# Four-block network on one core: GpSimd rounds the third and fourth input groups of the MLP to FP4 in place of VectorE

## The chip, the cores and the metric

The kernel runs on one core of a Trainium2 chip, as one launch. A core has TensorE (matmuls and transposes, results in PSUM), VectorE, ScalarE and GpSimd (elementwise work), and SyncE, which here issues the DMAs. Each engine runs its own queue of instructions in order and waits on semaphores for the others. The metric is the device time of one execution in microseconds.

## The reference

The input `x` (32 sequences of 64 tokens, width 128) passes four residual blocks: cross attention with rotary positions, a routed FFN (2 of 8 experts), cross attention by autocorrelation, and last the MLP that the change touches. Before each stands a layer norm, and each block's result is scaled by the tanh of a gate. The MLP quantises its inputs and weights to FP4 in blocks of 16 values, and multiplies:

```python
def fp4_quant_dequant(x):
    xb = x.reshape(shape[:-1] + (shape[-1] // BLOCK, BLOCK))
    scale = jnp.max(jnp.abs(xb), axis=-1, keepdims=True) / 6.0
    scale = jnp.maximum(scale, jnp.float32(1e-12))
    xn = xb / scale
    idx = jnp.searchsorted(_MID, jnp.abs(xn))
    q = _GRID[idx] * jnp.sign(xn) * scale
    return q.reshape(shape)
def fp4_linear(x, w):
    return jnp.einsum('bsk,nk->bsn', fp4_quant_dequant(x), fp4_quant_dequant(w))
...
gate = fp4_linear(x, w_gate)          # 128 -> 352
y = fp4_linear(x, w_up)
h = jax.nn.silu(gate) * y
return fp4_linear(h, w_down)          # 352 -> 128
```

## The kernel before

All work is scheduled by hand: every engine has one written-out order of steps, and semaphores tie the orders together. The 2048 tokens are 16 tiles of 128 tokens. In the MLP the inputs are quantised in four **groups** of four tiles (512 columns of a 128-partition buffer; the code counts them from 0, so the third and the fourth are groups 2 and 3), and the rest goes in eight **pairs** of two tiles (704 columns of h), counted from 0. The last two pairs are finished as four halves.

*A group's quantisation.* `x_scale` on VectorE takes the blocks' largest magnitudes (L285), their reciprocals (L286), and shrinks the values (L290, 128x512) so that the FP4 steps become steps of a float's own rounding. ScalarE takes magnitudes (`x_magnitude`, L734). `x_round` on VectorE rounds with two instructions of the same helper, `fp4_off` (L298): max(magnitude, 1.5) minus value, and max(magnitude, 1.5) minus that. GpSimd then scales back: `fp4_scale` (L294, 32 numbers) and `fp4_unscale` (L305, 128x512) in `x_unscale`. TensorE transposes the group (`turn_x`, L1601), ScalarE copies the transposes out of PSUM.

*A pair.* TensorE makes the gate product and the up product (`gate`, `up`, both on L1607), ScalarE the SiLU (L721). VectorE multiplies the two (L1090, from PSUM), takes the blocks' maxima (L1095), their reciprocals (L1101) and shrinks h (L290, 128x704). ScalarE takes magnitudes (L728), VectorE rounds with two instructions (L298, 128x704), one step later. GpSimd unscales (L294, L305, 128x704), TensorE transposes h (L1633) and makes the down product onto the residual (L1639, L1644), ScalarE copies the result out, and SyncE stores it.

VectorE's order in the MLP is: groups 0 and 1, then `pair_step(q)` for each pair q. A step q holds the product and the shrink of pair q and the roundings of pair q - 1. Between the maxima and the reciprocals of a step stand the odd jobs: `x_round(2)` in step 1, `x_scale(3)` in step 2, `x_round(3)` in step 3; `x_scale(2)` ends step 0. GpSimd's order is a loop over q from 1: in rounds 1 and 3 the unscale of group 2 or 3, then the scale of pair q - 1, then the unscale of pair q - 1, which waits for VectorE's roundings in step q. TensorE's order is `up(q+1)`, then turn and down product of pair q - 2, then `gate(q+2)`, and in rounds 1 and 3 the transposes of group 2 or 3.

Of the kernel before, what the change touches and what calls it, by code (L numbers as in the profile page):

```python
# [15 lines left out]
ALU = mybir.AluOpType  # L16
# [89 lines left out]
def build(nc, a):  # L106
    with ExitStack() as ctx:
# [21 lines left out]
        def carve(start, *shape):  # L129
            return shaped(region[:, start:start + int(np.prod(shape))], shape)  # L130
# [61 lines left out]
        qv, qm, qd, xqT = ([carve(k + 512 * i, 4 * D) for i in range(2)] for k in range(14336, 18432, 1024))  # L192
# [33 lines left out]
        x2_tr x2_done xn_c xn_c_late xn_c_dve xf_done xf_used q_done pp_done hs_done hs_read hs_turned cf_ready corr_done corr_read  # L226
        dve_c lead_ready lead_exp lags_ready lags_turned gt_ready g_done of_done
        y1_done y1_ready o_done x3_read x3_done
        floors_set hsc_ready xsc_ready rolled_made codes_set xn_d xn_d_dve xv_done xm_done xd_done xq_done xqt_done xqt_used gate_done gu_done sg_done hh_done hv_done hm_done hd_done hq_done hq_last ht_done ht_used dn_done x4_done out_done dve_d""".split()
        m = {n: ctx.enter_context(nc.semaphore(n)) for n in names}  # L230
        x_sem = [m["ld_x0"], m["ld_x1"]]
        w_sem = [m[f"w{i}"] for i in range(6)]
# [44 lines left out]
        def blocks(z):  # L277
            return z.rearrange("p (n k) -> p n k", k=BLK)

        def spread(z, nblk):  # L280
            return z.unsqueeze(2).broadcast_to([P, nblk, BLK])
# [6 lines left out]
        def fp4_shrunk(eng, out, src, inv):  # L288

            return eng.scalar_tensor_tensor(out, src, 6.0 / FINE * (1.0 - 2.0 ** -24), inv, ALU.mult, ALU.mult)  # L290

        def fp4_scale(eng, amax, sc):

            return eng.tensor_scalar(sc, amax, FINE / 6.0, None, ALU.mult)  # L294

        def fp4_off(eng, out, mag, z):

            return eng.scalar_tensor_tensor(out, mag, 1.5, z, ALU.max, ALU.subtract)  # L298

        def fp4_round(eng, st, v, mag, diff):  # L300
            st.step(fp4_off(eng, diff, mag, v))
            return fp4_off(eng, diff, mag, diff)

        def fp4_unscale(eng, diff, sc, nblk, out):
            return eng.tensor_tensor(blocks(out), blocks(diff), spread(sc, nblk), ALU.mult)  # L305
# [47 lines left out]
        def _(pool):  # L353
# [119 lines left out]
            def x_unscale(g):  # L473
                pool.wait_ge(m["xv_done"], g + 1)
                fp4_scale(pool, xmx[g % 2], xsc[g % 2]).then_inc(m["xsc_ready"], 1)
                pool.wait_ge(m["xd_done"], g + 1)
                pool.wait_ge(m["xsc_ready"], g + 1)
                fp4_unscale(pool, qd[g % 2], xsc[g % 2], 4 * D // BLK, qv[g % 2]).then_inc(m["xq_done"], 1)
# [10 lines left out]
            def h_scale(q):  # L489

                pool.wait_ge(m["hv_done"], q + 1)
                if q >= 3:
                    pool.wait_ge(m["hq_done"], q - 2)
                fp4_scale(pool, hmx[q % 3], hsc[q % 3]).then_inc(m["hsc_ready"], 1)

            for q in range(1, WHOLE + 1):
                u = (q - 1) % 2
                if q in (1, 3):
                    x_unscale((q + 3) // 2)
                h_scale(q - 1)  # L500
                pool.wait_ge(m["hd_done"], q)
                pool.wait_ge(m["hsc_ready"], q)
                if q >= 3:
                    pool.wait_ge(m["ht_done"], q - 2)
                fp4_unscale(pool, hd[u], hsc[(q - 1) % 3], 2 * NH, hq[u].rearrange("p a n -> p (a n)")).then_inc(m["hq_done"], 1)
# [289 lines left out]
        def _(dve):  # L795
# [267 lines left out]
            def x_scale(g):  # L1063

                u = g % 2
                dve.wait_ge(m["xn_d"], 4 * g + (2 if g else 4))
                if g == 1:
                    dve.wait_ge(m["xn_d_dve"], 2)
                if g >= 2:
                    dve.wait_ge(m["xqt_done"], g - 1)  # L1070
                    dve.wait_ge(m["xsc_ready"], g - 1)
                else:
                    dve.wait_ge(m["floors_set"], 3)
                nblk = 4 * D // BLK
                src = xb[:, nblk * g:nblk * (g + 1), :]
                fp4_inverse(dve, dd, src, xmx[u], xin[u])
                fp4_shrunk(dve, blocks(qv[u]), src[:, :, 0:BLK], spread(xin[u], nblk)).then_inc(m["xv_done"], 1)

            def x_round(g):
                dve.wait_ge(m["xm_done"], g + 1)  # L1080
                fp4_round(dve, dd, qv[g % 2], qm[g % 2], qd[g % 2]).then_inc(m["xd_done"], 1)

            def pair_step(q):

                u, w, n3 = q % 2, (q - 1) % 2, q % 3
                if q < PAIRS:
                    dve.wait_ge(m["sg_done"], q + 1)
                    dve.wait_ge(m["gu_done"], q + 1)
                    rows = "p a (n k) -> p a n k"
                    dve.tensor_tensor(hh[u].rearrange("p (a n) k -> p a n k", a=2), sg[u].rearrange(rows, k=BLK),  # L1090
                                      ps[:, 3:5, 0:MLP].rearrange(rows, k=BLK), ALU.mult).then_inc(m["hh_done"], 1)
                    if q >= 3:
                        dve.wait_ge(m["hq_done"], q - 2)
                    dve.wait_ge(m["hh_done"], q + 1)
                    k = dd.mark(dve.tensor_reduce(hmx[n3], hb[u], AX, ALU.max, apply_absolute_value=True))  # L1095
                    if q in (1, 3):
                        x_round((q + 3) // 2)
                    if q == 2:
                        x_scale(3)
                    dd.after(k)  # L1100
                    dd.step(dve.reciprocal(hin[n3], hmx[n3]))  # L1101
                    fp4_shrunk(dve, hh[u], hh[u], spread(hin[n3], 2 * NH)).then_inc(m["hv_done"], 1)
                    if q == 0:
                        x_scale(2)
                if 1 <= q <= WHOLE:
                    dve.wait_ge(m["hm_done"], q)
                    if q >= 3:
                        dve.wait_ge(m["hq_done"], q - 2)
                    dd.step(fp4_off(dve, blocks(hd[w]), blocks(hm[w]), hh[w]))
                    fp4_off(dve, hd[w], hm[w], hd[w]).then_inc(m["hd_done"], 1)  # L1110
# [23 lines left out]
            for q in range(PAIRS):  # L1134
                pair_step(q)
# [673 lines left out]
```

## Time and profile before

| what | value |
|---|---|
| median of 3 timed runs | 273.46 us (272.43, 273.46, 278.04) |
| the profiled execution, whole | 271.89 us |
| its span, first to last instruction | 270.1 us |
| TensorE matmul busy | 249.0 us, 92% |
| VectorE busy | 190.2 us, 70%, 494 instructions |
| ScalarE busy | 164.3 us, 61% |
| GpSimd busy | 125.0 us, 46%, 200 instructions |
| TensorE's granted clock, mean | 0.994 |

The shares are means over the four blocks, which have different bounds; the MLP is the last stage, from about 205 us on. Times in the rows below count from the start of the span. PE is TensorE, PEld its weight loads, DVE is VectorE, ACT is ScalarE, POOL is GpSimd. In a timeline, several instructions of one line are merged into one row with their count behind "x".

### The profile page before, as it was taken

To read this page: it belongs to the slowest core of one execution; us is meant where nothing else is said; L and a number is where in the kernel's file an instruction comes from. 1 tells how busy PE (TensorE), PEld (TensorE's weight loads), DVE (VectorE), ACT (ScalarE), POOL (GpSimd) and SP (SyncE) were. 2 spreads that over 40 slices of the span, in tenths; PEclk is the share of its full clock that TensorE was granted. 3 is DMA by queue.
4 is the path that set the end of the run, shared out by engine and by line. 5 is a ranking of instruction groups with operands and counts; after the bars stand their busy time and mean duration, and the time that the engine had idled before them with its cause. 6 is when DMAs were issued, how large, how long until landed. Compare 5 with 4: busy or idle time off the path is not lost.

```text
span 270.1 us, 6349 instructions
## 1 busy us (share of the span) xinstructions
PE 249.0 (92%) x2204; PEld 197.5 (73%) x2204; DVE 190.2 (70%) x494; ACT 164.3 (61%) x382; POOL 125.0 (46%) x200
## 2 busy tenths in 40 slices
PE   8999999999798989999999999979999864999886
PEld 6656477777576868999999999765699532667675
DVE  4899588888999764352222222796686999999993
ACT  2369996666478656686566667474448683353543
POOL 4475579999601403219992220267004534252220
PEclk9999999999999999999999999999999999899999
DMA  6999100000000118876777772000000000000111
GB/s 192 380 344 410 40 4 2 2 4 0 2 2 4 31 56 340 362 290 285 290 301 287 291 296 81 0 4 0 4 0 2 1 0 0 0 21 23 39 40 40
DMA packets 12384, 30.19 MB, mean 112 GB/s; under 512 B 1088, under 2 KB 5440, under 8 KB 12224
## 3 DMA queue, kind: packets, MB, share of 16 engines
q1 hardware_dynamic: 12352, 29.78, 29.2%
q8 instruction: 18, 0.29, 0.5%
q14 instruction: 14, 0.11, 0.1%
HBM read 9.78 MB, written 1.05 MB: 40 GB/s over the span
## 4 chain that ended last, share of the span: by engine, by line
PE 58%; DVE 23%; issue 7%; ACT 5%; DMA 2%; SPq 1%; POOL 1%; DVEq 0%; ACTq 0%
PE ps L1420 12%; PE ps L1409 11%; DVE s_region L298 5%; PE ps L1252 5%; PE ps L1226 5%; PE ps L1239 4%; PE ps L1159 3%; DVE s_region L1090 3%; PE ps L1150 3%; DVE s_small L1095 2%; PE ps L1151 2%; PE ps L1262 2%; DVE s_region L290 2%; PE ps L1470 1%; DMA s_ctxT<-ctxT 1%
## 5 line engine op out<-in xcount | busy, mean ns | idle before, releaser
L635 ACT ACTIVATE s_region<-ps,s_region 128x128 f32<-128x128 f32 x144 | 41.0, 369 | 21.8 <-PE ps L1409 21.7
L965 DVE SCALAR_TENSOR_TENSOR s_ctxT<-ps,s_region,s_ctxT 128x64 f32 x72 | 18.1, 282 | 43.9 <-PE ps L1420 43.9
L1409 PE MATMUL ps<-s_region 128*128 128x128 f32 x288 | 38.2, 276 | 0.2 <-DMA s_region<-s_wall 0.2
L1420 PE MATMUL ps<-s_region 128*128 128x128 f32 x288 | 37.9, 275 | 0.0
L1409 PEld LDWEIGHTS ps<-s_region 128*128 128x128 f32 x288 | 35.0, 192 | 0.7 <-DMA s_region<-s_wall 0.3
L1420 PEld LDWEIGHTS ps<-s_region 128*128 128x128 f32 x288 | 35.0, 192 | 0.2 <-issue 0.2
L430 POOL COPY s_region<-s_xt 128x64 f32 x72 | 14.8, 236 | 31.0 <-PE ps L1409 23.3
L1607 PE MATMUL ps<-s_region 128*128 128x352 f32 x64 | 22.4, 491 | 6.2 <-DVE s_region L1090 3.9
L575 ACT COPY s_region<-ps 128x512 f32<-128x512 f32 x32 | 17.2, 592 | 15.1 <-PE ps L1239 15.1
L305 POOL TENSOR_TENSOR s_region<-s_region,s_small 128x704 f32<-128x704 f32 (+2 forms) x11 | 14.6, 1331 | 23.7 <-DVE s_region L298 23.5
L1252 PEld LDWEIGHTS ps<-s_region 128*64 128x64 f32 x512 | 16.3, 138 | 12.5 <-ACT s_region L575 10.7
L834 DVE TENSOR_REDUCE s_small<-ps 128x16 f32<-128x1024 f32 x16 | 19.6, 1225 | 8.0 <-PE ps L1226 7.9
L374 POOL TENSOR_SCALAR s_region<-s_region 128x512 f32<-128x512 f32 x16 | 24.7, 1569 | 0.1
L271 POOL TENSOR_SCALAR s_small<-s_small 128x4 f32<-128x4 f32 (+3 forms) x14 | 3.2, 231 | 44.4 <-DVE s_small L248 44.4
L1607 PEld LDWEIGHTS ps<-s_region 128*128 128x128 f32 x64 | 11.8, 198 | 13.2 <-DVE s_region L1090 5.4
L298 DVE SCALAR_TENSOR_TENSOR s_region<-s_region 128x704 f32<-128x704 f32 (+2 forms) x28 | 20.4, 728 | 0.7 <-ACT s_region L734 0.2
L842 DVE TENSOR_TENSOR s_region<-ps,s_small 128x1024 f32<-128x1024 f32 x16 | 19.5, 1216 | 0.1
L1252 PE MATMUL ps<-s_region 128*64 128x18 f32 x512 | 17.8, 212 | 1.2 <-DVE s_x L857 0.9
L1226 PE MATMUL ps<-s_region 64*64 64x512 f32 x128 | 17.4, 614 | 1.1 <-POOL s_region L374 1.1
L570 ACT ACTIVATE s_region<-s_region 128x1024 f32<-128x1024 f32 x16 | 17.0, 1063 | 0.7 <-DVE s_region L842 0.7
L1239 PE MATMUL ps<-s_par,s_region 128*128 128x128 f32 x128 | 16.7, 273 | 0.0
L273 POOL TENSOR_TENSOR s_small<-s_small,s_par 128x4 f32<-128x4 f32 (+3 forms) x14 | 16.3, 1163 | 0.0
(237 smaller groups left out, 523.3 us busy)
## 6 DMA issues: line engine op xcount, KB each, us to landing
s_region<-s_wall SPq DMA_DIRECT2D x36, 514.0 KB, 3.0
s_wall<-wall SPq DMA_DIRECT2D x8, 514.0 KB, 9.4
s_par<-par SPq DMA_DIRECT2D x1, 1280.0 KB, 10.4
s_x<-x SPq DMA_DIRECT2D x2, 512.0 KB, 6.7
out<-s_x SPq DMA_DIRECT2D x6, 128.0 KB, 1.9
s_region<-ffn SPq DMA_DIRECT2D x1, 560.0 KB, 3.6
s_ctxT<-ctxT SPq DMA_DIRECT2D x2, 256.0 KB, 4.1
s_ctxT<-ctxT SPq DMA_DIRECT2D x1, 512.0 KB, 6.6
```

The lines of the kernel that those rows point to most:

```text
L298: return eng.scalar_tensor_tensor(out, mag, 1.5, z, ALU.max, ALU.subtract)
L374: pool.tensor_scalar(kbd[g % 2][:, j, :], cols, hmask[:, j:j + 1], None, ALU.mult).then_inc(m["kbd_done"], 1)
L635: ins = act.activation(hg[j % 3][:, c, :], ps[:, j % 3, RPT * S * c:RPT * S * (c + 1)], ACT.Gelu, bias=wbuf[j % 6][:, FF + FC * D + c:FF + ...
L834: dve.tensor_reduce(mx[t % 2], scores(t % 2), AX, ALU.max).then_inc(m["mx_done"], 1)
L842: dve.tensor_tensor(ssub[t % 2], scores(t % 2), mx[t % 2].unsqueeze(2).broadcast_to([P, H, S]), ALU.subtract).then_inc(m["s_sub"], 1)
L965: dve.scalar_tensor_tensor(row, ps[:, 4 + j % 2, S * k:S * k + S], w, row, ALU.mult, ALU.add).then_inc(m["acc_done"], 1)
L1226: ins = mm(ps[S * row:S * row + S, 2 * (t % 2) + half, :], qT[rows, 2 * t + row, :], kbd[g % 2][rows, :, k:k + S], start=True, stop=True)
L1239: ins = tr(ps[:, 4 + half, P * k:P * k + P], pr[t % 2][:, c:c + P], ident)
L1252: ins = mm(ps[S * row:S * row + S, 6 + t % 2, n * c:n * c + n], pT[t % 2][:, c, S * row:S * row + S], vbd[:, 2 * t + row, c, :], start=Tru ...
L1409: ins = mm(ps[:, j % 3, RPT * S * c:RPT * S * (c + 1)], w[:, P * c:P * c + P], xg[j % 4], start=True, stop=True)
L1420: ins = mm(ps[:, 4 + j % 2, 0:RPT * S], w[:, FF + D * c:FF + D * c + D], hg[j % 3][:, c, :], start=(c == 0), stop=(c == FC - 1))
L1607: ins = mm(ps[:, 1 + 2 * n + t, 0:MLP], xqT[(q // 2) % 2][:, lo:lo + P], wguT[:, MT * P * n:MT * P * n + MLP], start=True, stop=True)
```

## The change

The two calls of `x_round` that stand inside VectorE's `pair_step` go. GpSimd gets a new function, `x_round_late`, called in rounds 1 and 3 of its loop directly before `x_unscale` of the same group. [...] Groups 0 and 1 stay on VectorE.

```diff
+            def x_round_late(g):
+
+                u, done = g % 2, 2 * (g - 2)
+                pool.wait_ge(m["xm_done"], g + 1)
+                pool.tensor_scalar(qm[u], qm[u], 1.5, None, ALU.max).then_inc(m["xr_done"], 1)
+                pool.wait_ge(m["xr_done"], done + 1)
+                pool.tensor_tensor(qd[u], qm[u], qv[u], ALU.subtract).then_inc(m["xr_done"], 1)
+                pool.wait_ge(m["xr_done"], done + 2)
+                pool.tensor_tensor(qd[u], qm[u], qd[u], ALU.subtract).then_inc(m["xd_done"], 1)
+
             for q in range(1, WHOLE + 1):
                 u = (q - 1) % 2
                 if q in (1, 3):
+                    x_round_late((q + 3) // 2)
                     x_unscale((q + 3) // 2)
                 h_scale(q - 1)
...
                     k = dd.mark(dve.tensor_reduce(hmx[n3], hb[u], AX, ALU.max, apply_absolute_value=True))
-                    if q in (1, 3):
-                        x_round((q + 3) // 2)
                     if q == 2:
                         x_scale(3)
                     dd.after(k)
```

## Rows read from the trace of the kernel before

**Rows 1.** Busy us by engine in one stretch of the MLP; then PEclk, DMA.

```profile
235.00:240.00 5.00, 4.55 (x26) 3.29 (x25) 4.83 (x7) 2.15 (x4) 3.25 (x4) 1.00 0.09 28
```

**Rows 2.** Chain of waits that ended last, from 215 us: start, us, what.

```profile
236.43 0.61 DVE s_region L298
...
237.06 0.69 DVE s_region L298
...
238.16 1.40 issue
...
265.74 0.55 PE ps L1655 x3
```

**Rows 3.** Timeline of VectorE, 221 to 257 us: start, us, line, operation.

```profile
223.05 1.41 DVE L298 SCALAR_TENSOR_TENSOR s_region<-s_region 128x512 f32<-128x512 f32 x2
224.37 0.42 DVE L1101 RECIPROCAL s_small<-s_small 128x44 f32<-128x44 f32 x1
224.83 1.52 DVE L290 SCALAR_TENSOR_TENSOR s_region<-s_region,s_small 128x704 f32<-128x704 f32 x1
226.27 1.83 DVE L298 SCALAR_TENSOR_TENSOR s_region<-s_region 128x704 f32<-128x704 f32 x2
228.01 0.88 DVE L1090 TENSOR_TENSOR s_region<-s_region,ps 128x704 f32<-128x704 f32 x1
...
230.91 0.69 DVE L290 SCALAR_TENSOR_TENSOR s_region<-s_region,s_small 128x512 f32<-128x512 f32 x1
...
234.51 0.88 DVE L1090 TENSOR_TENSOR s_region<-s_region,ps 128x704 f32<-128x704 f32 x1
...
241.31 0.88 DVE L1090 TENSOR_TENSOR s_region<-s_region,ps 128x704 f32<-128x704 f32 x1
...
243.72 0.89 DVE L290 SCALAR_TENSOR_TENSOR s_region<-s_region,s_small 128x704 f32<-128x704 f32 x1
...
246.26 0.88 DVE L1090 TENSOR_TENSOR s_region<-s_region,ps 128x704 f32<-128x704 f32 x1
...
256.17 0.88 DVE L1090 TENSOR_TENSOR s_region<-s_region,ps 128x704 f32<-128x704 f32 x1
```

**Rows 4.** Timeline of GpSimd, 221 to 257 us; in brackets idle time before.

```profile
224.54 1.06 POOL L305 TENSOR_TENSOR s_region<-s_region,s_small 128x512 f32<-128x512 f32 x1 [2.78 <-DVE s_region L298]
225.68 0.85 POOL L294 TENSOR_SCALAR s_small<-s_small 128x44 f32<-128x44 f32 x1
228.18 1.38 POOL L305 TENSOR_TENSOR s_region<-s_region,s_small 128x704 f32<-128x704 f32 x1 [1.65 <-DVE s_region L298]
229.65 0.32 POOL L294 TENSOR_SCALAR s_small<-s_small 128x44 f32<-128x44 f32 x1
```

**Rows 5.** Two lines early in the kernel (L820, L382): ns min/median/max, first and last start.

```profile
L820 DVE TENSOR_SCALAR s_region<-s_region x4: 477/480/1493, 16.7 to 17.9; 128x512 f32<-128x512 f32 x4
...
L382 POOL TENSOR_TENSOR s_region<-s_region x6: 1268/1276/1498, 9.3 to 26.4; 128x512 f32<-128x512 f32 x6
```

**Rows 6.** GpSimd's instructions by line and shape: count, busy us, mean ns.

```profile
L374 POOL TENSOR_SCALAR s_region<-s_region 128x512 f32<-128x512 f32 x16 | 24.7, 1569 | 0.1
...
L400 POOL TENSOR_TENSOR s_region<-s_region 128x512 f32<-128x512 f32 x2 | 2.6, 1280 | 0.2
```

**Rows 7.** Timeline of ScalarE, 221 to 257 us: the two groups' magnitudes.

```profile
221.40 0.63 ACT L734 ACTIVATE s_region<-s_region 128x512 f32<-128x512 f32 x1
...
233.86 0.62 ACT L734 ACTIVATE s_region<-s_region 128x512 f32<-128x512 f32 x1
```

**Rows 8.** Timeline of TensorE, 221 to 257 us: transposes, and products of pairs.

```profile
225.65 0.66 PE L1601 MATMUL ps<-s_par,s_region 128*128 128x128 f32 x4 [0.80 <-POOL s_region L305]
228.95 2.71 PE L1607 MATMUL ps<-s_region 128*128 128x352 f32 x4 [2.64 <-DVE s_region L1090]
...
252.20 2.53 PE L1607 MATMUL ps<-s_region 128*128 128x352 f32 x8
```

**Rows 9.** Busy us by engine from 228 to 232 us, columns as above.

```profile
228.00:232.00 4.00, 3.05 (x8) 1.95 (x9) 3.86 (x8) 0.28 (x1) 1.71 (x2) 0.57 0.00 0
```

More of the change, by code:

```diff
@@ L228, in build @@
         y1_done y1_ready o_done x3_read x3_done
-        floors_set hsc_ready xsc_ready rolled_made codes_set xn_d xn_d_dve xv_done xm_done xd_done xq_done xqt_done xqt_used gate_done gu_done sg_done hh_done hv_done hm_done hd_done hq_done hq_last ht_done ht_used dn_done x4_done out_done dve_d""".split()
+        floors_set hsc_ready xsc_ready rolled_made codes_set xn_d xn_d_dve xv_done xm_done xd_done xr_done xq_done xqt_done xqt_used gate_done gu_done sg_done hh_done hv_done hm_done hd_done hq_done hq_last ht_done ht_used dn_done x4_done out_done dve_d""".split()
         m = {n: ctx.enter_context(nc.semaphore(n)) for n in names}
```

## The prediction

> **What bounds the kernel now.** I read three views in this order. First the busy time by stretch: in the MLP VectorE works 4.83 of every 5.00 us while GpSimd works 3.25 [rows 1]. Second the chain of waits over the last stage: up to 265.74 us each step on it is VectorE's (or its issue), the two roundings that the change moves stand there with 0.61 and 0.69 us, and only at 265.74 does TensorE follow [rows 2]. Third the timelines of VectorE and GpSimd against each other [rows 3, 4]. The reader is to see the distance from one SwiGLU product (L1090) to the next. A plain step, 241.31 to 246.26, takes 4.95. The step with the fourth group's rounding, 234.51 to 241.31, takes 6.80. The excess of 1.85 has two parts. One is the rounding itself. The other is a stall: the shrink on L290, 0.89 alone (243.72), takes 1.52 at 224.83 because GpSimd's unscale of the inputs runs until 225.60; the chain shows the same stall again as 1.40 of "issue" at 238.16 [rows 2, 3, 4]. So the stall is 0.63 and the rounding, net of what it covered, 1.85 - 0.63 = 1.22.
>
> VectorE is the bound, so 1.22 twice, 2.4 us, looks free to take. With the stall twice it is 3.7 us. Even this upper end is 1.4% of the time, under the 2% that a measurement of this kernel can tell from no change (the three times shown lie 272.43 to 278.04).
>
> **What is removed.** Two scalar_tensor_tensor of 128x512 in each of two steps: 1.41 us for a pair [rows 3], 1.22 net as above. VectorE also no longer waits for the magnitudes of these groups.
>
> **What is added.** On GpSimd, three instructions for each group. Subtractions of two full 128x512 operands exist in the trace: 1.28 each (L400) [rows 6]. A maximum against a constant does not; the nearest row is the multiply L374 of the same size at 1.57, and I take that. Its bounds are 0.5 (what VectorE needs for a tensor_scalar of this size, 0.48 [rows 5]) and 1.9 (a little over L374). With gaps of 0.08 between dependent instructions, as between 225.60 and 225.68 [rows 4], that is 1.57 + 1.28 + 1.28 + 3 x 0.08 = 4.4 us of GpSimd to replace 1.4 of VectorE. GpSimd has idle time for that in number (3.16 per plain step). Its new wait is for ScalarE's magnitude, and queued behind it are the scale and unscale of the group, the scale of h and the unscale of h that TensorE transposes. The third group's magnitude is there at 222.03 and the fourth's at 234.48 [rows 7].
>
> **What the added work meets.** This decides the sum. At 224.83 a VectorE instruction with two operands in SBUF stood still until GpSimd's ended and then ended 0.74 later (225.60 to 226.34). GpSimd's small scale issued at 225.68 stood still in turn and ended 0.19 after 226.34; alone it takes 0.32 (229.65), so it entered 0.13 before VectorE's end [rows 3, 4]. Early in the kernel the same goes both ways: a VectorE tensor_scalar of 0.48 took 1.49, a GpSimd tensor_tensor of 1.28 took 1.50 [rows 5]. Against this, GpSimd's unscale of h at 228.18 (1.38) lies beside the product L1090, which reads PSUM, and a reduction, and neither side is longer [rows 3, 4]. So the two engines exclude each other on some forms: VectorE's shrink and its two roundings of h (L290, L298 twice: 2.7 of the 4.95 us) against any sizeable GpSimd instruction here.
>
> The Trainium skill, "SBUF — State Buffer", section "Who interferes with whom", says it as a rule: a VectorE instruction with two SBUF inputs contends with a GpSimd instruction that reads SBUF, and whichever issues first holds the shared ports for its whole instruction. The rows above agree (1.52 for 0.89), and by that rule the maximum holds them as well, which gives the upper of the two ends worked out below; without it the change would simply save its 2.4 us.
>
> Now the working by the rows, third group. Maximum 222.10 to 223.67. VectorE's reciprocal moves 1.22 up, from 224.37 to 223.15, and the shrink is issued at 223.61, ahead of the first subtraction (issued 223.75), and ends at 224.50. First subtraction ends 224.50 + 1.28 - 0.13 = 225.65. First rounding of h: 225.65 + 0.74 = 226.39. Second subtraction: + 1.15 = 227.54. Second rounding: 228.28; the next product starts 0.08 before that, 228.20, against 228.01 now: 0.19 *later*. The 1.22 and the 0.63 are spent. GpSimd goes on: scale until 228.47, unscale (1.06) until 229.61, scale of h until 230.01, unscale of h 230.09 to 231.47. It now meets the shrink of the last input group (230.91 + 0.19 [rows 3]) and delays it by some 0.2. Third group: +0.4.
>
> Fourth group. Product of step 3 at 234.9, unscale of h 235.1 to 236.5, maximum 236.5 to 238.1. The shrink is issued at 237.3. If the maximum excludes it, it ends 238.1 + 0.74 = 238.85; first subtraction 240.00, rounding 240.74, second subtraction 241.89, rounding 242.63, next product 242.55 against 241.31: +1.24. Then scale, unscale (to 243.96), scale of h, and unscale of h 244.44 to 245.82, which falls onto the next shrink (issued 244.96, ends 245.82 + 0.74 = 246.56 in place of 245.85): +0.71. Together +1.95. If the maximum does not exclude the shrink, this ends at 238.2 and the same counting gives +1.4 when the subtraction gets in first, +0.8 when VectorE does. From step 4 on GpSimd is back beside the product. The sum lies between +0.8 and +1.95; I take +1.5, a little above the middle since the small scale at 225.68, a one-input form like the maximum, was seen to be excluded [rows 4].
>
> What is late next: the inputs' unscale ends at 229.61 in place of 225.60, so the transposes that started at 225.65 start 4.0 later, and the up product behind them at 230.3 or more in place of 228.95: TensorE is about 1.4 late [rows 4, 8]. Its last gate and up products end at 252.20 + 2.53 = 254.73 for the VectorE product at 256.17 [rows 3, 8]; VectorE itself is 1.5 later, so 1.4 us of cover remain. No DMA is moved, and the output queue only follows.
>
> **The sum.** 271.89 (the profiled execution: span 270.1 and 1.8 around it) + 1.5 = 273.4. This execution is 1.57 under the median of the three timed ones; the middle of all four is 272.9, and from there I forecast 274.4.
>
> **Rivals.** *A gain.* The subtractions do not keep VectorE out, or lose every race and run beside product and reduction. For it: VectorE's second rounding at 226.27 was not visibly longer although the small scale waited beside it (1.83 for two) [rows 3, 4]. Against it: 1.52 for 0.89. It would save 2.4 to 3.7, but TensorE then binds: its products for 256.17 end at 254.73, 1.44 before, and its transposes, after 222.10 + 4.4 + 0.4 + 1.06 = 228.0, let it start only some 0.3 earlier. So -1.8: 271.1.
>
> *Nothing left over.* The roundings go, and the collisions cost what they cost, within half a microsecond: VectorE wins the races (the +0.8 end, and a shorter maximum, below 1.0 us, under the reduction). 272.9.
>
> *Slower, TensorE binds.* The mechanism is the granted clock. Around the end of 2.64 us of idle it stands at 0.57 from 228 to 232, near its lower level of 1.2 GHz, and the up product takes 2.71 [rows 8, 9] against 2.53 for two products at full clock: nearly twice as slow. With the change TensorE is idle from 224.9 to 229.6. If the low level then lasts over the following turn, down and gate as well, that step's 4.5 us of matmuls (4.55 of 5.00 busy [rows 1]) grow by some 3, TensorE is 4.5 late and no longer 1.4, and passes its cover of 1.4 from there on. It decides as soon as TensorE is over 2.9 late: +1.95 + 2 = +3.9, 276.8. Against it: by 235 us the clock is at full again [rows 1].
>
> **How the numbers follow.** Forecast 0.62 (274.4), gain 0.15 (271.1), nothing left over 0.13 (272.9), TensorE binds 0.10 (276.8). The likeliest's own range is 273.2 to 275.4. The range reaches to the others: 270.7 to 277.2, leaving out less than a tenth on either side for the spread of the timings. Faster by over 2% (under 268.0) nothing here reaches: 0.02. Slower by over 2% (over 278.9) would need all 8.8 us of added GpSimd work less 2.4 on the path, or a timing like 278.04: 0.04. Within 2%: 0.94.
>
> **What would show it.** Right: in the changed profile the shrink and the roundings of h in steps 1 and 3 take 1.5 to 1.9 us each in place of 0.9, with ends 0.7 behind the ends of GpSimd's subtractions; the subtractions themselves show 1.5 to 2; steps 1 and 3 still take 6.7 us or more, and step 4 more than 4.95; VectorE's busy time stays near 190 although four instructions are gone. Wrong: steps 1 and 3 near 5 us; VectorE idle before L1090 on a TensorE matmul; or a maximum far from 1.57.

## The result, and the profile after

The changed kernel takes 273.75 us (median of 20 runs, 272.67 to 279.86) against 272.18 for the kernel before (20 runs). The ratio, which compares the faster executions of both alone (seven of the changed kernel's took 276.85 us or more, at a mean granted clock of about 0.975 in place of 0.987 or more), is 1.0049, 95% interval 1.0031 to 1.0067: 1.3 us slower, within the 2% and on the side that was forecast (+1.5). The profiled execution has a span of 272.0 us in place of 270.1. Of these 1.9 us, 0.33 lie ahead of the change: the product of step 1 starts at 221.62 in place of 221.29. The rest, 1.55, is in steps 1 to 4.

The timeline of VectorE in the changed kernel (start, us, line, operation); L1101 is the product, L1106 and L1110 the maxima and reciprocals of h, L290 the shrink, L298 the roundings:

```profile
221.62 0.88 DVE L1101 TENSOR_TENSOR s_region<-s_region,ps 128x704 f32<-128x704 f32 x1
...
223.97 0.89 DVE L290 SCALAR_TENSOR_TENSOR s_region<-s_region,s_small 128x704 f32<-128x704 f32 x1
224.78 3.82 DVE L298 SCALAR_TENSOR_TENSOR s_region<-s_region 128x704 f32<-128x704 f32 x2
228.52 0.88 DVE L1101 TENSOR_TENSOR s_region<-s_region,ps 128x704 f32<-128x704 f32 x1
...
231.41 1.05 DVE L290 SCALAR_TENSOR_TENSOR s_region<-s_region,s_small 128x512 f32<-128x512 f32 x1
...
235.37 0.88 DVE L1101 TENSOR_TENSOR s_region<-s_region,ps 128x704 f32<-128x704 f32 x1
...
237.78 0.89 DVE L290 SCALAR_TENSOR_TENSOR s_region<-s_region,s_small 128x704 f32<-128x704 f32 x1
238.59 3.84 DVE L298 SCALAR_TENSOR_TENSOR s_region<-s_region 128x704 f32<-128x704 f32 x2
242.36 0.88 DVE L1101 TENSOR_TENSOR s_region<-s_region,ps 128x704 f32<-128x704 f32 x1
...
244.76 1.71 DVE L290 SCALAR_TENSOR_TENSOR s_region<-s_region,s_small 128x704 f32<-128x704 f32 x1
...
258.05 0.88 DVE L1101 TENSOR_TENSOR s_region<-s_region,ps 128x704 f32<-128x704 f32 x1
```

And GpSimd's in the same kernel; L500 is the maximum of the magnitudes with 1.5, L502 the magnitudes minus the values, L504 the magnitudes minus that (each waits for the one before), L305 the unscales:

```profile
222.45 1.50 POOL L500 TENSOR_SCALAR s_region<-s_region 128x512 f32<-128x512 f32 x1 [4.19 <-ACT s_region L745]
224.04 1.95 POOL L502 TENSOR_TENSOR s_region<-s_region 128x512 f32<-128x512 f32 x1
226.06 1.79 POOL L504 TENSOR_TENSOR s_region<-s_region 128x512 f32<-128x512 f32 x1
...
230.53 1.39 POOL L305 TENSOR_TENSOR s_region<-s_region,s_small 128x704 f32<-128x704 f32 x1
...
236.90 1.49 POOL L500 TENSOR_SCALAR s_region<-s_region 128x512 f32<-128x512 f32 x1
238.47 1.33 POOL L502 TENSOR_TENSOR s_region<-s_region 128x512 f32<-128x512 f32 x1
239.88 1.81 POOL L504 TENSOR_TENSOR s_region<-s_region 128x512 f32<-128x512 f32 x1
...
244.34 1.39 POOL L305 TENSOR_TENSOR s_region<-s_region,s_small 128x704 f32<-128x704 f32 x1
```

Step 3 of the kernel before had these in VectorE's timeline:

```profile
238.12 1.51 DVE L290 SCALAR_TENSOR_TENSOR s_region<-s_region,s_small 128x704 f32<-128x704 f32 x1
239.56 1.83 DVE L298 SCALAR_TENSOR_TENSOR s_region<-s_region 128x704 f32<-128x704 f32 x2
```

Read them side by side. The 128x512 roundings are gone from VectorE, and the stall of the shrink in these steps too (0.89 and 0.89 in place of 1.52 [rows 3] and 1.51). In their place the pair of roundings of h takes 3.82 and 3.84 in place of 1.83: each waits for one of GpSimd's subtractions. The subtraction at 224.04 ends at 225.99, and VectorE's first rounding, issued at 224.78, takes 1.96 and ends at 226.74, 0.75 behind it. GpSimd waits in turn: 1.95, 1.79 and 1.81 for a subtraction of 1.28; only the one at 238.47, issued 0.12 ahead of VectorE's rounding, took 1.33. Later the unscale of h, which used to lie beside the product [rows 4], falls onto a shrink: at 230.53 onto that of the last input group (1.05 for 0.69), at 244.34 onto that of step 4 (1.71 for 0.89).

TensorE's timeline in the changed kernel, and its clock from 228 to 236 us (the last number but two):

```profile
230.02 1.11 PE L1610 MATMUL ps<-s_par,s_region 128*128 128x128 f32 x4 [4.83 <-POOL s_region L305]
230.93 2.55 PE L1616 MATMUL ps<-s_region 128*128 128x352 f32 x4
...
237.09 2.53 PE L1616 MATMUL ps<-s_region 128*128 128x352 f32 x8
...
254.50 2.53 PE L1616 MATMUL ps<-s_region 128*128 128x352 f32 x8
```

```profile
228.00:236.00 8.00, 5.94 (x19) 4.07 (x20) 7.83 (x11) 1.79 (x3) 4.64 (x6) 0.57 0.00 0
```

It idles 4.83 us, and its clock is near the lower level (a mean of 0.57 of full speed) for 8 us and no longer 4 [rows 9]. The gate and up products of pair 4, now at 237.09, started at 234.77 in the kernel before:

```profile
234.77 2.53 PE L1607 MATMUL ps<-s_region 128*128 128x352 f32 x8
```

But its last products end at 257.03, 1.0 before VectorE's product at 258.05, and VectorE waits for nothing: 4.83 of 5 us busy as before.

### The profile page after: what moved, and what is told of

It reads as the page before. It is cut to its first block, busy times and chain, and to the rows that moved or that the text cites. A ratio compares the mean times of both kernels' runs of the same rounds, so it can differ in the third digit from the quotient of the medians.

```text
span 272.0 us, 6351 instructions
## 1 busy us (share of the span) xinstructions
PE 250.0 (92%) x2204; PEld 198.2 (73%) x2204; DVE 191.7 (70%) x490; ACT 164.3 (60%) x382; POOL 136.0 (50%) x206
## 3 DMA queue, kind: packets, MB, share of 16 engines
HBM read 9.78 MB, written 1.05 MB: 40 GB/s over the span
## 4 chain that ended last, share of the span: by engine, by line
PE 58%; DVE 23%; issue 8%; ACT 5%; DMA 3%; SPq 1%; POOL 1%; DVEq 0%; ACTq 0%
PE ps L1429 12%; PE ps L1418 11%; DVE s_region L298 5%; PE ps L1261 5%; PE ps L1235 5%; PE ps L1248 4%; PE ps L1168 3%; DVE s_region L1101 3%; PE ps L1159 3%; DVE s_small L1106 2%; PE ps L1160 2%; PE ps L1271 2%; DMA s_ctxT<-ctxT 1%; PE ps L1479 1%; DVE s_region L290 1%
## 5 line engine op out<-in xcount | busy, mean ns | idle before, releaser
L298 DVE SCALAR_TENSOR_TENSOR s_region<-s_region 128x704 f32<-128x704 f32 (+2 forms) x24 | 21.7, 903 | 0.6 <-ACT s_region L745 0.2
L305 POOL TENSOR_TENSOR s_region<-s_region,s_small 128x704 f32<-128x704 f32 (+2 forms) x11 | 14.7, 1333 | 13.4 <-DVE s_region L298 12.7
```

## The experiments

From each trace I took the starts of VectorE's products and their distances, steps 1 to 6, in us (the sums are taken from product 1 to product 7, since product 1 itself starts between 220.48 and 224.72 us in these executions, because of differences ahead of the change):

| kernel | 1 | 2 | 3 | 4 | 5 | 6 | sum | less before | ratio of times |
|---|---|---|---|---|---|---|---|---|---|
| before | 6.73 | 6.50 | 6.80 | 4.95 | 4.95 | 4.95 | 34.88 | | |
| changed | 6.90 | 6.85 | 6.98 | 5.79 | 4.95 | 4.95 | 36.43 | +1.55 | 1.0049 |
| third group only | 6.90 | 6.84 | 6.80 | 4.95 | 5.30 | 4.95 | 35.75 | +0.87 | 1.0049 |
| same, padded | 6.91 | 6.85 | 6.80 | 4.95 | 4.95 | 4.95 | 35.41 | +0.53 | 1.0022 |
| fourth group only | 6.73 | 6.49 | 6.98 | 5.79 | 5.30 | 4.95 | 36.24 | +1.36 | 1.0065 |
| rounding left out | 4.88 | 6.49 | 5.55 | 4.95 | 4.95 | 4.94 | 31.77 | -3.11 | 0.9895 |
| one-input in place | 5.29 | 7.72 | 5.52 | 6.84 | 5.23 | 5.52 | 36.12 | +1.24 | 1.0042 |
| unscale later | 6.08 | 6.50 | 6.15 | 4.99 | 4.95 | 4.95 | 33.62 | -1.26 | 0.9944 |
| turns between | 6.73 | 6.49 | 6.98 | 4.95 | 4.95 | 4.95 | 35.05 | +0.17 | 1.0013 |
| changed, turns between | 6.91 | 6.85 | 6.98 | 5.78 | 4.95 | 4.95 | 36.42 | +1.54 | 1.0137 |
| same again | 6.91 | 6.85 | 5.90 | 6.29 | 5.23 | 5.52 | 36.69 | +1.81 | 1.0064 |

**The change in halves.** First the third group alone on GpSimd, then the fourth alone; VectorE keeps the other's rounding.

```diff
                 if q in (1, 3):
-                    x_round_late((q + 3) // 2)
+                    if q == 1:
+                        x_round_late(2)
                     x_unscale((q + 3) // 2)
...
+                    if q == 3:
+                        x_round(3)
```

> Only the third group is rounded on GpSimd; the fourth stays on VectorE. Theory (the two engines exclude each other on instructions with two SBUF operands): in the changed kernel steps 1 and 2 of VectorE were longer than before by 0.18 and 0.35 us, so this kernel is 0.5 us slower than before (ratio 1.002), steps 3 and 4 being 6.8 and 4.95 again. Rival (TensorE is late and at half clock after its 4.8 us of idle, which only the third group causes): the whole 1.5 us are here, ratio 1.005 to 1.006, with VectorE idle before a product.

> Only the fourth group is rounded on GpSimd. Theory (exclusion): steps 3 and 4 are longer by 0.2 and 0.8 us, so 1.0 us slower than before (ratio 1.004). Rival (TensorE): TensorE's idle time and clock around 228 us are as before, so no change (1.000).

Measured: 1.0049 (1.0024 to 1.0075) and 1.0065 (1.0045 to 1.0085), both over the 1.002 and 1.004 of the theory; the rival asked for everything in the first and nothing in the second. The first time alone would suit the rival too; the second does not, and by steps the theory holds to 0.04: 1 and 2 are longer by 0.17 and 0.34 in the first kernel, 3 and 4 by 0.18 and 0.84 in the second. What is over is the same in both, 0.35 in step 5. The timeline of VectorE with the fourth group alone shows it as idle time before the reduction L1107 (in brackets), which stands 0.10 behind the product in the other steps:

```profile
247.18 0.88 DVE L1102 TENSOR_TENSOR s_region<-s_region,ps 128x704 f32<-128x704 f32 x1
248.51 0.93 DVE L1107 TENSOR_REDUCE s_small<-s_region 128x44 f32<-128x748 f32 x1 [0.46 <-DVE s_region L1102]
```

The product that the reduction waits for ended at 248.06. Both kernels have two VectorE instructions fewer than the kernel before. So the third-group kernel was run with two memsets at the start of VectorE's program:

```diff
             st = Steps(dve, m["dve_a"])
+            for n in range(2):
+                dve.memset(pad[:], 0.0).then_inc(m["padded"], 1)
+                dve.wait_ge(m["padded"], n + 1)
```

> The kernel with only the third group on GpSimd again, with two small memsets and their waits put at the very start of VectorE's program, so that it has as many instructions as before the change. The two kernels that move one group showed a pause of 0.35 us on VectorE before the reduction of step 5 that the trace puts to no wait. If the pause hangs on where that instruction lies in VectorE's program, it is gone, step 5 takes 4.95, and the time is 0.5 us over before (ratio 1.002). If it hangs on the moved work, step 5 takes 5.30 again (1.003 to 1.005).

Step 5 is 4.95 again and the ratio 1.0022 (1.0003 to 1.0041), as expected. As far as one trace of each kernel shows, the pause hangs on where an instruction lies in VectorE's program, not on the moved work; what it is made of stays open. The third group costs 0.5 us.

**What the work is worth on VectorE.** Nobody rounds:

```diff
-                    if q in (1, 3):
-                        x_round((q + 3) // 2)
...
-                pool.wait_ge(m["xd_done"], g + 1)
+                pool.wait_ge(*((m["xd_done"], g + 1) if g < 2 else (m["xm_done"], g + 1)))
...
-                fp4_unscale(pool, qd[g % 2], ...)
+                fp4_unscale(pool, (qd if g < 2 else qm)[g % 2], ...)
```

> Neither engine rounds the third and fourth groups; GpSimd scales back the unrounded magnitudes, so this part of the quantisation is missing. It shows what taking the work from VectorE is worth with nothing put onto GpSimd. Theory: VectorE loses the 1.22 us of rounding and the 0.63 us of stall in each of steps 1 and 3, which become 5.0 us long; 3 us faster than before in all (ratio 0.989), somewhat under 3.7 since TensorE has little room. Rival (TensorE binds the MLP as it stands): 1.4 us at most (0.995), with VectorE idle before products.

0.9895 (0.9876 to 0.9914), 2.9 us faster. TensorE does not hold it back: VectorE waits for none of its products. So the three instructions of each group on GpSimd cost about 1.3 + 2.9 = 4.2 us of the path (4.7 by the steps) for 8.4 us of work (twice 1.50 + 1.28 + 1.28 and gaps); about half of it was hidden. Step 3 keeps a stall: GpSimd's unscale still meets the shrink, 1.47 in VectorE's timeline of this kernel, while step 1's stands free:

```profile
227.07 0.89 DVE L290 SCALAR_TENSOR_TENSOR s_region<-s_region,s_small 128x704 f32<-128x704 f32 x1
...
238.51 1.47 DVE L290 SCALAR_TENSOR_TENSOR s_region<-s_region,s_small 128x704 f32<-128x704 f32 x1
```

**Which GpSimd instructions shut VectorE out.** The subtractions become maxima that read one operand:

```diff
-                pool.tensor_tensor(qd[u], qm[u], qv[u], ALU.subtract)
+                pool.tensor_scalar(qd[u], qm[u], 1.5, None, ALU.max)
...
-                pool.tensor_tensor(qd[u], qm[u], qd[u], ALU.subtract)
+                pool.tensor_scalar(qd[u], qd[u], 1.5, None, ALU.max)
```

> As the changed kernel, but GpSimd's two subtractions are replaced by maxima against a constant on the same tiles, of the same 128x512 size, which read one operand: the values are not rounded, the number, place and length (1.5 us) of GpSimd's instructions are kept or grow. Theory (only two-operand GpSimd instructions shut VectorE out, since the maximum at 236.90 left the shrink of 0.89 alone): VectorE's roundings of h go from 3.8 us a pair back to 1.8, steps 1 and 3 to 5.0; what is left is TensorE, whose inputs come 4 us late, so the time is between 1.5 us less and 0.5 more than before (0.994 to 1.002). Rival (any sizeable GpSimd instruction shuts VectorE out): the pair takes 4 us or more, and the time is 1.5 to 2.5 us over before (1.006 to 1.009).

1.0042 (1.0027 to 1.0057): the time missed both. The pairs of L298 missed the theory by little (2.22 and 2.09 for 1.81) and the rival by far. VectorE's timeline, then GpSimd's, in this kernel:

```profile
224.12 2.22 DVE L298 SCALAR_TENSOR_TENSOR s_region<-s_region 128x704 f32<-128x704 f32 x2
...
230.22 2.10 DVE L290 SCALAR_TENSOR_TENSOR s_region<-s_region,s_small 128x704 f32<-128x704 f32 x1
...
236.39 1.17 DVE L290 SCALAR_TENSOR_TENSOR s_region<-s_region,s_small 128x704 f32<-128x704 f32 x1
```

```profile
223.39 2.17 POOL L502 TENSOR_SCALAR s_region<-s_region 128x512 f32<-128x512 f32 x1
...
230.18 1.39 POOL L305 TENSOR_TENSOR s_region<-s_region,s_small 128x704 f32<-128x704 f32 x1
...
236.21 1.49 POOL L500 TENSOR_SCALAR s_region<-s_region 128x512 f32<-128x512 f32 x1 [0.67 <-ACT s_region L745]
```

So the theory was too simple. A maximum that starts at 236.21 delays the shrink issued 0.18 later by 0.28 (1.17) and not until its own end at 237.70; in the changed kernel a shrink issued 0.88 after the maximum's start, at 237.78, took 0.89. Of each pair of roundings, too, the one issued behind a maximum's beginning is late by some 0.4 and 0.3 (1.30 and 1.18 for 0.89) and still ends before the maximum does. In these traces a one-input instruction shuts VectorE out at its beginning only, a two-input one until its end; and VectorE's two-input instruction holds up either (2.17 for 1.50). The 1.5 to 1.6 us that steps 1 and 3 gain on the changed kernel are nearly all given back where the late unscales, which read two operands, fall onto shrinks: 2.10 in step 2 and a step 4 of 6.84. Then TensorE is late too (VectorE's timeline of this kernel, idle time and who ended it in brackets):

```profile
251.57 0.89 DVE L1101 TENSOR_TENSOR s_region<-s_region,ps 128x704 f32<-128x704 f32 x1 [0.20 <-PE ps L1616]
...
257.09 0.89 DVE L1101 TENSOR_TENSOR s_region<-s_region,ps 128x704 f32<-128x704 f32 x1 [0.48 <-PE ps L1616]
```

**TensorE's part.** The transposes of the third and fourth groups move from before an up product to between the residual and the down product of the next step; once alone on the kernel before, as a control, and once on the changed kernel. ScalarE's copy of these transposes moves with them, to behind its copy of the transposes of h (not shown in the cut), and so ahead of the next magnitudes.

```diff
-                if q in (1, 3):
-                    turn_x((q + 3) // 2)
...
-                    down(q - 2)
+                    down(q - 2, q // 2 + 1 if q in (2, 4) else None)   # turn_x inside, before its wait for hT
```

> The kernel before with the move of TensorE's transposes alone, as a control. VectorE's order and GpSimd's are untouched, so by the theory that VectorE sets the time: no change (1.000). Rival (TensorE's order matters): faster by up to 1 us.

> The changed kernel with the same move of TensorE's transposes: the up product of pair 3 no longer stands behind transposes that wait for GpSimd, TensorE idles less around 225 to 230 us, and its clock falls for a shorter time or not. Theory (exclusion alone costs the time): steps as in the changed kernel, 1.5 us slower than before (ratio 1.005 to 1.006). Rival (the late transposes and the half clock cost part of it): 0.5 to 1.5 us of it come back (1.000 to 1.004).

The control is 1.0013 (0.9996 to 1.0029), no change that can be told. Its step 3 is 0.17 longer all the same: ScalarE's magnitude of the fourth group now ends at 236.03, and VectorE's rounding waits for it until 236.06. The changed kernel with the move had steps equal to the changed kernel's within 0.01, although TensorE's gate product of step 4 starts at 235.70 in place of 237.09 and its clock is back at full speed by 234 us. So neither the order nor the clock of TensorE was in them. Its ratio, 1.0137 (1.0092 to 1.0183), lies over both expectations and is wide, because two of its six executions lay some 3 us over the others. No trace of these two was kept, so what held them up stays open; the kernel was run again.

> The changed kernel with TensorE's transposes moved, once more, since its first times were few and lay far apart (273.6 to 277.4). Theory (exclusion alone costs the time): as the changed kernel, 1.004 to 1.007. Rival (late transposes and half clock): 1.000 to 1.003.

1.0064 (1.0035 to 1.0092): nothing comes back, as the theory has it. But this profiled execution went another way. VectorE's timeline, then GpSimd's:

```profile
238.29 2.76 DVE L298 SCALAR_TENSOR_TENSOR s_region<-s_region 128x704 f32<-128x704 f32 x2
...
244.45 2.89 DVE L298 SCALAR_TENSOR_TENSOR s_region<-s_region 128x704 f32<-128x704 f32 x2
...
252.49 0.89 DVE L1103 TENSOR_TENSOR s_region<-s_region,ps 128x704 f32<-128x704 f32 x1 [0.20 <-PE ps L1618]
...
258.01 0.89 DVE L1103 TENSOR_TENSOR s_region<-s_region,ps 128x704 f32<-128x704 f32 x1 [0.47 <-PE ps L1618]
```

```profile
236.83 1.49 POOL L500 TENSOR_SCALAR s_region<-s_region 128x512 f32<-128x512 f32 x1 [0.21 <-ACT s_region L745]
238.41 1.90 POOL L502 TENSOR_TENSOR s_region<-s_region 128x512 f32<-128x512 f32 x1
```

GpSimd's first subtraction was issued at 238.41, just behind VectorE's rounding at 238.29, and lost the race; step 3 was 0.9 shorter than before the change. The trace shows why: TensorE's clock stood at 0.50 to 0.67 until 236 us (in the first run of this kernel it was at full speed from 234 us on), the moved transposes and ScalarE's work behind them came later, and the maximum waited 0.21 for the magnitude, which started at 236.13 (235.46 in the first run). The rest of GpSimd's work moved on by a step, the unscale of h came late, TensorE's transposes of h waited 2.24 us for it, and VectorE then waited 0.20 and 0.47 for TensorE. The last product starts at 258.01, in the changed kernel at 258.05. So TensorE stands right behind VectorE as the next bound.

**A version without the stall.** If the exclusion also explains the 0.63 us of stall in the kernel before, VectorE can keep the rounding, and GpSimd's unscale of the inputs has only to move beside instructions that do not conflict: behind the unscale of h. TensorE's transposes move as above to give it time.

```diff
                 fp4_unscale(pool, hd[u], ...).then_inc(m["hq_done"], 1)
+                if q in (1, 3):
+                    x_unscaled((q + 3) // 2)      # was ahead of the scale and unscale of h
```

> The kernel before (VectorE rounds), with GpSimd's unscale of the third and fourth groups moved behind the unscale of h of the same round, so that it lies beside VectorE's product, reductions and reciprocals; and TensorE's transposes of the group moved from before the next up product to between the residual and the down product of the following step, where TensorE waits for ScalarE. Theory (exclusion): the shrinks of steps 1 and 3 go from 1.52 back to 0.89, steps 2 and 4 grow by 0.0 to 0.2; 1.1 us faster than before (ratio 0.996). Rival (the 0.63 are something else in these steps): no change.

0.9944 (0.9904 to 0.9984), 271.0 us against 271.9: faster than the kernel before, and so than the changed one. Its VectorE, and its GpSimd with the two unscales merged into one row:

```profile
225.63 0.89 DVE L290 SCALAR_TENSOR_TENSOR s_region<-s_region,s_small 128x704 f32<-128x704 f32 x1
...
238.28 0.89 DVE L290 SCALAR_TENSOR_TENSOR s_region<-s_region,s_small 128x704 f32<-128x704 f32 x1
...
243.23 0.91 DVE L290 SCALAR_TENSOR_TENSOR s_region<-s_region,s_small 128x704 f32<-128x704 f32 x1
```

```profile
228.33 2.40 POOL L305 TENSOR_TENSOR s_region<-s_region,s_small 128x704 f32<-128x704 f32 x2 [5.37 <-DVE s_region L298]
...
240.98 2.40 POOL L305 TENSOR_TENSOR s_region<-s_region,s_small 128x704 f32<-128x704 f32 x2 [3.62 <-DVE s_region L298]
```

The shrinks of steps 1 and 3 are 0.89 again, both steps 0.65 shorter, and step 4 costs 0.04. The move of the transposes alone, in the control, brought no such gain.

## Why the prediction was right

- *VectorE is the bound.* Right: with its rounding left out and nothing added, the kernel is 2.9 us faster.
- *The added work excludes VectorE's two-operand instructions.* Right, and the forecast's mechanism: pairs of roundings of 3.8 us, their ends 0.75 behind the subtractions', step 1 longer by 0.17 (0.19 forecast), step 4 by 0.84 (0.71). The one-input kernel takes most of it away in steps 1 and 3. Of the signs that were named, one failed: the shrinks of these steps took 0.89, not 1.5 to 1.9. The Trainium skill's rule ("SBUF — State Buffer", "Who interferes with whom") holds for the subtractions. For the maximum it says more than the runs show: a shrink beside it took 0.89 in the changed kernel and 1.17 in the one-input kernel.
- *The sum between +0.8 and +1.95, +1.5 taken.* The trace has +1.55, the times +1.3. That these lie so near +1.5 is luck in part, for the sum is made up differently. The upper end rested on the maximum shutting out the shrink of step 3; it did not. By the working without that, with the subtraction first, the sum was +1.4 (its own steps, worked again, give 1.3), and that is what happened, by a race that the subtraction won by 0.12 us; the reason I gave for going above the middle, the small scale that waited at 225.68, showed VectorE holding up GpSimd and not the reverse. The collision with the last input group's shrink was sized at 0.2 and is 0.36 (1.05 for 0.69). The maximum was 1.50 for 1.57. The forecast of 274.4 lies 0.65 over the median of 273.75 because its base did: 272.9 from four executions, 272.18 from twenty.
- *TensorE is about 1.4 late, with 1.4 of cover left.* The mechanism is right, the size short: its gate product of step 4 starts at 237.09 in place of 234.77, 2.0 late after the 0.33 ahead of the change, with a mean clock of 0.57 until 236; cover left at the last product is 1.0.
- *The rivals.* The gain was capped at 1.8 by TensorE. The kernel without rounding gained 2.9, so the 1.44 of cover in the cap was no fixed limit: TensorE's chain moves forward with the product it waits for. But that kernel lacks GpSimd's added work too, so the rest of the cap, the late transposes of the inputs, stays untested; nothing in the forecast hung on it. "Nothing left over" by VectorE winning a race was seen once (step 3 of 5.90). What it won was lost again, in step 4 to further collisions (6.29) and in steps 5 and 6 to TensorE (5.23 and 5.52), which had waited for the late unscale of h; the prediction had looked only at the inputs' transposes.

## What to carry to other kernels

Before moving elementwise work from VectorE to an idle GpSimd, list which of both engines' instructions read two operands from SBUF and lay them over each other in the timeline. In these traces GpSimd's idle time was free for a two-operand instruction only where VectorE read PSUM, reduced or took reciprocals. Here those places were in part taken by the unscale of h, so 8.4 us of moved work cost 4.2 on the path against 2.9 saved. The same map shows the cheaper move: shift the GpSimd instruction that already collides.

A one-input `tensor_scalar` of VectorE belongs on the list too. In the kernel before, one of 128x4 took 0.81 in place of 0.17, ending just after GpSimd's unscale that ran beside it. VectorE's timeline of the kernel before, then GpSimd's:

```profile
212.91 0.17 DVE L251 TENSOR_SCALAR s_small<-s_small 128x4 f32<-128x4 f32 x1
...
215.67 0.81 DVE L251 TENSOR_SCALAR s_small<-s_small 128x4 f32<-128x4 f32 x1
```

```profile
215.40 1.06 POOL L305 TENSOR_TENSOR s_region<-s_region,s_small 128x512 f32<-128x512 f32 x1
```

## What the runs showed that I had not expected

- A one-input GpSimd instruction of 1.5 us delays a two-operand VectorE instruction only if that is issued near its start: by 0.28 at 0.18 behind it, by nothing at 0.65 (the last run of the changed kernel with moved transposes) and at 0.88.
- A one-input maximum of 128x512 takes GpSimd 1.50 us, longer than a subtraction of two operands, 1.28.
- Two instructions fewer in VectorE's program came with a pause of 0.35 us at one instruction of step 5, and with two memsets at the start it was gone.
